# A graph layer with residual and layer norm: nine small tiles allocated behind the large ones

## The reference

```python
# x (32, 256, 512) float32, adj (32, 256, 256) int32, weight, wq, wk (512, 512)
output = jnp.einsum('bni,io->bno', x, weight)
q = jnp.einsum('bni,io->bno', x, wq)
k = jnp.einsum('bni,io->bno', x, wk)
alpha = jnp.einsum('bno,bmo->bnm', q, k)
alpha = jnp.maximum(alpha, 0.0) * (adj != 0)
alpha = jax.nn.softmax(alpha, axis=1)
y = x + jnp.einsum('bnm,bmo->bno', alpha, output)
m, v = mean(y, axis=-1), var(y, axis=-1)
return (y - m) / jnp.sqrt(v + 1e-5)
```

## Time and profile before

| what | value |
|---|---|
| median of 3 runs | 565.71 us (565.19 to 566.07) |
| span of the profiled execution | 564.6 us |
| PE busy | 552.3 us, 98% |
| PEld busy | 463.7 us, 82% |
| DVE busy | 288.6 us, 51% |
| ACT busy | 226.8 us, 40% |
| DMA | 62.03 MB, mean 110 GB/s |

### The profile page before, as it was taken

The page is one execution under the profiler, slowest core; times in us unless marked ns, Lnnn a source line. Parts: engine busy times, 40 slices in busy tenths (PEclk is TensorE's granted clock), DMA queues, the critical chain, the costliest instruction groups (busy, mean ns, idle before and its releaser), DMA issues.

```text
span 564.6 us, 7382 instructions
## 1 busy us (share of the span) xinstructions
PE 552.3 (98%) x2736; PEld 463.7 (82%) x2736; DVE 288.6 (51%) x678; ACT 226.8 (40%) x529; POOL 18.3 (3%) x24
## 2 busy tenths in 40 slices
PE   5999999999999999999999999999999999999995
PEld 4888888888888888888888888888888888888884
DVE  3635555554545445455454555445454554545356
ACT  4534433443434344332543434344343533443153
POOL 0000000000000000000000000000000000000002
PEclk9999999999999999999999999999999999999998
DMA  8902141342504234250343414134250432121003
GB/s 292 377 1 109 66 144 57 113 149 87 176 11 159 92 111 149 74 177 9 115 145 111 149 40 146 74 111 149 74 186 3 147 110 111 74 74 74 0 1 149
DMA packets 23628, 62.03 MB, mean 110 GB/s; under 512 B 1216, under 2 KB 1216, under 8 KB 21696
## 3 DMA queue, kind: packets, MB, share of 16 engines
q1 hardware_dynamic: 23616, 61.87, 31.0%
HBM read 45.09 MB, written 16.78 MB: 110 GB/s over the span
## 4 chain that ended last, share of the span: by engine, by line
PE 97%; DMA 1%; DVE 1%; ACT 0%; POOLq 0%; POOL 0%; issue 0%
PE t_bank L197 11%; PE t_bank L196 11%; PE t_bank L198 11%; PE v_bank L197 10%; PE v_bank L196 10%; PE v_bank L198 10%; PE s_bank L196 6%; PE s_bank L198 6%; PE s_bank L197 6%; PE o_bank L198 5%; PE o_bank L197 5%; PE o_bank L196 5%; PE v_bank L236 1%; PE t_bank L236 1%; DMA xt<-in_x_t 1%; DVE y L474 0%
## 5 line engine op out<-in xcount | busy, mean ns | idle before, releaser
L196 PE MATMUL t_bank<-xt_hi,g_hi 128*128 128x512 f32 x256 | 101.4, 396 | 0.0
L198 PE MATMUL t_bank<-xt_hi,g_lo 128*128 128x512 f32 x256 | 101.3, 396 | 0.0
L197 PE MATMUL t_bank<-xt_lo,g_hi 128*128 128x512 f32 x256 | 101.3, 396 | 0.0
L197 PE MATMUL v_bank<-w_lo,xt_hi 128*128 128x512 f32 x240 | 94.9, 395 | 0.0
L196 PE MATMUL v_bank<-w_hi,xt_hi 128*128 128x512 f32 x240 | 94.9, 395 | 0.0
L198 PE MATMUL v_bank<-w_hi,xt_lo 128*128 128x512 f32 x240 | 94.8, 395 | 0.0
L426 DVE TENSOR_TENSOR t_lo<-t_bank,t_hi 128x512 fp32r<-128x512 f32 x64 | 44.2, 691 | 97.1 <-ACT t_hi L346 97.0
L364 ACT ACTIVATE squares<-y,neg_mean 128x512 f32<-128x512 f32 x64 | 45.5, 712 | 90.6 <-DVE neg_mean L480 87.2
L346 ACT CAST t_hi<-t_bank 128x512 fp32r<-128x512 f32 x64 | 37.5, 586 | 106.9 <-PE t_bank L198 106.9
L426 DVE TENSOR_TENSOR v_lo<-v_bank,v_hi 128x512 fp32r<-128x512 f32 x62 | 42.8, 691 | 70.6 <-ACT v_hi L342 70.6
L342 ACT CAST v_hi<-v_bank 128x512 fp32r<-128x512 f32 x62 | 36.3, 586 | 97.1 <-PE v_bank L198 97.1
(11 more groups left out here) (70 smaller groups left out, 713.1 us busy)
## 6 DMA issues: line engine op xcount, KB each, us to landing
xn<-in_x SPq DMA_DIRECT2D x16, 1024.0 KB, 5.3
xt<-in_x_t SPq DMA_DIRECT2D x15, 1024.0 KB, 7.0
out<-y SPq DMA_DIRECT2D x15, 1024.0 KB, 5.2
adj<-in_adj_t SPq DMA_DIRECT2D x16, 512.0 KB, 3.3
xt<-in_x_t SPq DMA_DIRECT2D x4, 256.0 KB, 5.0
y<-in_w SPq DMA_DIRECT2D x4, 256.0 KB, 5.1
y<-in_wq_t SPq DMA_DIRECT2D x1, 1024.0 KB, 9.0
wk_raw<-in_wk_t SPq DMA_DIRECT2D x1, 1024.0 KB, 11.2
```

Of the source, the lines that this page charges most:

```text
L196: nc.tensor.matmul(dst, a[0], b[0], start=first, stop=False)
L197: nc.tensor.matmul(dst, a[0], b[1], start=False, stop=False)
L198: return nc.tensor.matmul(dst, a[1], b[0], start=False, stop=last)
```

## The change

The `sb(...)` lines of the nine statistics tiles move behind that of wk_raw. No instruction is added, removed or moved: on each engine the built program has the same rows in the same order. Only addresses differ, as in the table above: squares moves by 192 bytes, the seven tiles g_hi to wk_raw move by 288 bytes and now begin on a multiple of 128 bytes, and the small tiles go to the end.

```diff
         p_lo = sb("p_lo", [P, R, N], F32R)
-        neg_max = sb("neg_max", [P, R])
-        exp_sum = sb("exp_sum", [P, R])
-        inv_sum = sb("inv_sum", [P, R])
-        y_sum = sb("y_sum", [P, R])
-        neg_mean = sb("neg_mean", [P, R])
-        square_sum = sb("square_sum", [P, R])
         squares = sb("squares", [P, R, D])
-        var_eps = sb("var_eps", [P, R])
-        rstd = sb("rstd", [P, R])
-        minus_half = sb("minus_half", [P, R])
 
         g_hi = sb("g_hi", [P, K, D], F32R)
         g_lo = sb("g_lo", [P, K, D], F32R)
...
         wk_raw = sb("wk_raw", [P, K, D])
+        neg_max = sb("neg_max", [P, R])
+        exp_sum = sb("exp_sum", [P, R])
+        inv_sum = sb("inv_sum", [P, R])
+        y_sum = sb("y_sum", [P, R])
+        neg_mean = sb("neg_mean", [P, R])
+        square_sum = sb("square_sum", [P, R])
+        var_eps = sb("var_eps", [P, R])
+        rstd = sb("rstd", [P, R])
+        minus_half = sb("minus_half", [P, R])
```

## The result

The changed kernel takes 555.29 us (median of 5 runs, 555.0 to 556.07) where the kernel before took 565.71 us (median of 5, 565.19 to 566.42): ratio 0.982, 95% interval 0.981 to 0.983. That is faster, by 10.4 us or 1.8%; the forecast was 555.2 us. The range held it, and the price per matmul was right. The reason given for it was not, as the experiments show: it is not each tile's own address that counts, and the grid is not 128 bytes.

The account below looks back on a forecast made before the run. PE's distances between matmul starts were taken as the bound. T 5.1, V 4.8, G 0.3 and First V 0.2 us, 10.5 us in all, came off the 564.6 us span; with 1.1 us added, 555.2 us, range 554.3 to 557.1.

Parts of the forecast that it names:

- What bounds the kernel: From first data to last matmul, PE's distances between matmul starts make up the time; PE waits only twice, 6.1 and 0.3 us.
- The price, 6.67 ns a matmul: Each 512-column matmul in T, V, G and fast First V drops from 233.3 to 226.7 ns.
- O's steady pitch: The last 18 of O's 24 matmuls start 226.7 ns apart; this was taken as the pitch after the change.
- the upper bound: O's first six matmuls are slow because T's ahead of them are; ending that gains 14 x 0.03 = 0.4 us more.
- The count, 1570: Matmuls that gain: T 768, V 720, G 48, First V 34, together 10.5 us; O and S gain 0.
- an operand off the 128-byte grid, on either side, goes with 6.7 ns more: In V, T and G, one stationary or moving tile at 32 mod 128 adds 6.7 ns to each matmul.
- The rival of colliding streams: Weight load and moving stream collide at equal remainders; T, V and G rise 6.67 ns a matmul, 576.2 us; chance 0.03.
- One role only: Only the moving side pays (V, G, First V gain 5.3 us) or only the stationary (T, 5.1 us); 560.5 us, chance 0.04.
- The rule of the skill: Warm matmul distance is columns at 2.4 GHz plus about 2.5 ns, without an address term; change worth nothing, 565.7 us.
- No change, for O's data or its place: O is fast for its data, six matmuls per bank, or g, w, wk lying above 164000; 565.7 us, chance 0.09.
- Nothing else moved: VectorE and ScalarE changes, such as squares' writes, stay off the path, and the end moves as a whole: worth nothing.

Follow-up runs that it names:

- e1: Kernel after the change with 32 bytes of padding ahead of g_hi and 96 ahead of w_hi, so g_hi and g_lo begin at 32 mod 128: 564.51 us.
- e9: Kernel before the change with 32 bytes of padding ahead of xt_hi and 224 ahead of xn; g, w, wk and xt all at 32 mod 256: 555.09 us.
- e3: Kernel after the change with 32 bytes of padding ahead of every tile, so every matmul operand lies at 32 mod 128: 555.5 us.
- e8: Kernel before the change with 32 bytes of padding ahead of xt_hi and 96 ahead of xn, leaving xt 128 bytes from g and w mod 256: 566.5 us.
- e5: Kernel after the change, padded to stationary-to-moving distances mod 1024 of 256 in T and V, 384 in G, 128 in O: 557.42 us.
- e2: Kernel after the change with 32 bytes of padding ahead of w_hi and 96 ahead of wk_hi, so w_hi and w_lo begin at 32 mod 128: 561.14 us.
- e6: Kernel after the change, padded to stationary-to-moving distances of 16 bytes in T and V, 8 in G, 4 in O: 568.74 us.
- e12: Kernel after the change, padded to stationary-to-moving distances mod 256 of 96 in T, 160 in V, 252 in G, 64 in O: 568.1 us.

## Why the prediction was right, and where its reason was not

- **What bounds the kernel.** Right. PE's distances between starts make up the time, before and after, with the same two waits.
- **The price, 6.67 ns a matmul.** Right: T went from 11.20 to 10.88 us, to the last hundredth of a microsecond. Taking O's steady pitch, not its mean of 227.9 ns, was right: O's six slow matmuls were no part of its own price, and the changed kernel has O at 5.44 us. They are not simply the slow T's either, as the upper bound had it. In e1 T is slow and O takes 5.44 us; in e9 T is fast and O takes 5.47 us, because p is loaded beside a stream at another remainder.
- **The count, 1570.** Right for T, G and the 34 of First V. For V the price was too high by 0.03 us a stage, because each V comes behind an S and its first five matmuls stay slow: 4.4 us in place of 4.8. O's 0.34 us, which the sum had put at 0, makes this up almost exactly. That the time came out within 0.1 us of the forecast is therefore partly luck; each of the two terms was 0.3 to 0.4 us off.
- **The step that failed** is the inference "an operand off the 128-byte grid, on either side, goes with 6.7 ns more". The rows excluded form, banks, data in part and transfers, and left the addresses; but the address of one tile and the distance between two fit the rows of before equally well, since every fast stage there had both tiles at the same remainder and every slow one had just one of them moved. e3 (all tiles at 32, fast) and e9 (g, w and xt at 32, fast) decide for the distance, and e1, e8 and e5 put the period at 256 bytes and not 128. The forecast survived this by luck, because the table of addresses was kept as it is: all large tiles have sizes that are multiples of 256 bytes, so putting them behind one another brings the distance to 0 mod 256 along with the grid.
- **The rival of colliding streams** used the right quantity, the distance between the two streams, with the wrong sign. Equal remainders are the best case, not the worst. No run came near its 576.2 us.
- **One role only.** Excluded: e1 slows T by its stationary tile, e2 slows V by its moving one.
- **The rule of the skill.** The Trainium skill, page "TensorE: Matmul & The Clock Gate", section "Wait — 56ns, not 53.3ns?", has no term for an address, and the measurement decides against that here: the same instructions take 233.4 or 226.7 ns by a distance of 32 bytes (T before and after). At the slow clock its other half does agree with this trace: starts 0.43 us apart are 512 columns at 1.2 GHz with nothing on top, at a distance of 32 bytes in the kernel before as at 0 in the one after.
- **No change, for O's data or its place.** Excluded: O is slow with v moved by 128 bytes (e5), and T and V are fast with g and w still above 164000 in the partition (e9). O's six matmuls per bank were the same in e5 as well.
- **Nothing else moved.** Right: VectorE, ScalarE and the end behind the last matmul are the same within 0.5 us of busy time.

## What to carry to other kernels

Where TensorE is the bound and float32r operands stream beside 128-column weight loads, look at the distance between the start of the stationary and of the moving slice, mod 256 bytes: 0 gives 226.7 ns for 512 columns in a steady stage, every other distance tried 230 to 238 ns. Where one stage follows another, look also at the first load of the next beside the last stream of this one. A few small tiles allocated between large ones are enough to lose it, and one odd tile in a group of three costs all three. And when the rows of one kernel leave "addresses" as the cause, ask whether they tell one address from the distance of two, before a rule is written down.

## What the runs showed of the hardware that was not expected

- A distance that is no multiple of 16 bytes can cost more: 237.7 ns at 4 bytes (O in e6), though 230.0 ns at 252 (second half of G in e12), the least of all distances but 0.
- S, with 256 moving columns, was put down to its weight loads at 120 ns. In e9, with xt at 32 and t at 0, it takes 5.68 us in place of 5.75 (96.60 to the next V at 102.28), 118.3 ns a matmul: a distance other than 0 is slightly better there. 16 x 0.07 = 1.2 us of the span, which more than makes up for what G, T and O take more (0.9 us) and, with 0.2 us less ahead of G, puts e9 at 553.0 us of span beside 553.5. It does not carry to e8, with 32 against 128 between the two, where S takes 5.76.
- A stage that follows S starts with five slow matmuls (233, 236, 229, 233 and 231 ns on average in the kernel after, in place of 226.7) before it falls into its pitch, even with all distances at 0. They are nearly the same five as behind the odd load in e9.
